# Layer norm with four neighbouring nodes to a partition, flat group buffers, earlier self copies and an earlier release of the second stage

## The reference, cut to what matters

```python
def layer0(x):                                   # GIN with batch norm
    agg = segment_sum(x[src], dst)
    z = relu(((1 + eps) * x + agg) @ W1 + b1) @ W2 + b2
    z = (z - mean(z, axis=0)) * rsqrt(var(z, axis=0) + 1e-5) * gamma + beta
    return z + x
def layer1(x):                                   # graph convolution
    return relu(segment_sum(edge_weight * x[dst], src) @ W3)
x = layernorm(x + layer0(x))                     # over the 256 features of a node
x = layernorm(x + layer1(x))
```

## Time and profile before

| | us |
|---|---|
| median of 3 runs | 4353.71 (4353.64 to 4358.59) |
| the profiled execution, its own time | 4363.42 |
| its span | 4361.6 |
| POOL busy | 3205.9 (74%) |
| PE busy | 3410.1 (78%) |
| DVE busy | 2603.8 (60%) |
| ACT busy | 413.7 (9%) |

### The profile page before, as it was taken

How to read it: one execution, slowest core, us unless ns; L and a number is a source line. 1 busy time by engine, 2 the same in 40 slices (tenths; PEclk the granted TensorE clock), 3 DMA queues, 4 the chain that set the end, 5 groups by cost and what they waited for, 6 DMA issues and landing times.

```text
span 4361.6 us, 69515 instructions
## 1 busy us (share of the span) xinstructions
PE 3410.1 (78%) x16117; PEld 2809.4 (64%) x16118; DVE 2603.8 (60%) x5750; ACT 413.7 (9%) x1049; POOL 3205.9 (74%) x3456
## 2 busy tenths in 40 slices
PE   2887877877887787778536888888888888888887
PEld 2776766666676676667435666666666666666666
DVE  3987877877888788788374434344334344344343
ACT  0000000000000000000151000000000000000001
POOL 6777777777777777777626777777777777777775
PEclk6998988988989898898758999999999999999998
DMA  4344444444444444444683343433434434434343
GB/s 146 114 119 118 121 118 116 121 118 119 118 118 117 119 120 119 115 121 118 189 288 108 113 118 117 119 117 118 120 115 120 120 115 120 120 115 119 115 120 99
DMA packets 305380, 540.19 MB, mean 124 GB/s; under 512 B 85290, under 2 KB 197790, under 8 KB 305326
## 3 DMA queue, kind: packets, MB, share of 16 engines
q0 software_dynamic: 159424, 434.52, 34.4%
q10 hardware_dynamic: 90884, 70.85, 5.3%
q1 hardware_dynamic: 55018, 34.16, 2.6%
HBM read 489.80 MB, written 46.88 MB: 123 GB/s over the span
## 4 chain that ended last, share of the span: by engine, by line
POOL 65%; issue 22%; PE 7%; DMA 3%; POOLq 1%; DVE 1%; ACT 1%; ACTq 0%; SPq 0%; DVEq 0%; PEldq 0%
POOL ring L612 32%; POOL ring L545 32%; PE ps L1290 3%; PE ps L1498 2%; DMA x_dram<-ring 1%; PE ps L1373 1%; DMA ring<-x_dram,idx 1%; POOLq L621 1%; DMA ring<-in_x,idx 1%; DMA z_dram<-z_pair 1%; ACT ring L1731 1%; POOL ring L558 0%; POOLq L622 0%; PE ps L1340 0%; POOLq L396 0%
## 5 line engine op out<-in xcount | busy, mean ns | idle before, releaser
L545 POOL DMA_INDIRECT ring<-in_x,idx x1664 | 1593.4, 958 | 504.2 <-issue 473.3
L612 POOL DMA_INDIRECT ring<-x_dram,idx x1612 | 1528.5, 948 | 551.3 <-issue 490.2
L1498 PE MATMUL ps<-ring,work 128*128 x6448 | 1523.7, 391 | 342.2 <-SPq L521 339.8
L1498 PEld LDWEIGHTS ps<-ring,work 128*128 128x128 f32 x6448 | 1218.4, 193 | 633.1 <-issue 475.2
L1160 DVE TENSOR_SCALAR work<-ps,dstT,wT 128x256 f32<-128x256 f32 x1612 | 741.8, 534 | 1134.0 <-PE ps L1498 1068.6
L1290 PE MATMUL ps<-ring,ones_sb 128*128 x3324 | 913.5, 423 | 362.9 <-SPq L454 325.0
L1290 PEld LDWEIGHTS ps<-ring,ones_sb 128*128 128x128 f32 x3324 | 679.0, 211 | 513.4 <-issue 413.3
L1373 PEld LDWEIGHTS ps<-work 128*128 128x128 f32 x3384 | 429.3, 197 | 18.5 <-DVE work L882 3.7
L1373 PE MATMUL ps<-work 128*128 128x128 f32 x3384 | 427.9, 279 | 2.5 <-DVE work L882 2.5
L897 DVE SCALAR_TENSOR_TENSOR ones_sb<-ps,tile_base,dstT 128x256 f32<-128x256 f32 (+1 forms) x294 | 311.7, 1099 | 57.3 <-PE ps L1273 31.9
L877 DVE TENSOR_TENSOR work<-ps,current 128x768 f32<-128x768 f32 x282 | 266.6, 945 | 10.8 <-PE ps L1373 10.8
(11 more groups left out here) (240 smaller groups left out, 2123.7 us busy)
## 6 DMA issues: line engine op xcount, KB each, us to landing
ring<-in_x,idx POOLq DMA_INDIRECT x1664
ring<-x_dram,idx POOLq DMA_INDIRECT x1612
z_dram<-z_pair ACTq DMA_DIRECT2D x49, 256.0 KB
ones_sb<-x_dram ACTq DMA_DIRECT2D x49, 256.0 KB, 3.6
ring<-z_dram SPq DMA_DIRECT2D x24, 512.0 KB, 5.8
ring<-in_x SPq DMA_DIRECT2D x24, 512.0 KB, 7.1
x_dram<-ring ACTq DMA_DIRECT2D x24, 512.0 KB, 3.7
out<-ones_sb ACTq DMA_DIRECT2D x48, 256.0 KB
```

The lines of the kernel that those rows point to most:

```text
L545: nc.gpsimd.indirect_dma_start(out=ring[:, q, c, :], out_offset=None, in_=x, in_offset=bass.IndirectOffsetOnAxis(ap=idx[:, q, c:c + 1], ax ...
L612: nc.gpsimd.indirect_dma_start(out=ring[:, q, c, :], out_offset=None, in_=x1_dram, in_offset=bass.IndirectOffsetOnAxis(ap=idx[:, q, c:c + ...
L1498: last = nc.tensor.matmul(to[:, t * D:(t + 1) * D], ones_of[:, b, c, t * P:(t + 1) * P], ring[:, ds((p + b) & (RING - 1), 1), c, :].rearra ...
```

## The change

- **Self copies**: in the first round POOL copies the first two quarters' self weights after 32 gathers, and each later quarter's behind its own gathers, in place of all four behind the 64th.
- **Four neighbours**: in a group, partition p holds the nodes 4p to 4p + 3 (2p, 2p + 1 in the last group), so that x is loaded and x1 stored in pieces of 4 KB. The group buffers are flat in the ring's memory. z stays transposed in z_dram, two pairs to a group: keep_z writes pieces of 2 KB, a group's load reads 4 KB a partition. PE picks every fourth column when it turns z back.
- **Slots**: group g uses slot (g + 7) mod 8.
- **Square root**: ACT takes one square root at its start; the batch norm's square root stands ahead of the last keep_z.
- **Second stage**: PE gives the credit for s_added2 at its start, not after W3; ACT loads W3 in the first stage, behind the loads of the staged lists.

```diff
-        z_group = tiles[:, 0:XBUFS * GROUP, :]
-        x_group = tiles[:, XBUFS * GROUP:2 * XBUFS * GROUP, :]
+        ring_flat = ring_rows[:, :, :, :].rearrange("p a c d -> p (a c d)")
+        z_group = ring_flat[:, 0:XBUFS * GROUP * D].rearrange("p (g m f n) -> p g m f n", g=XBUFS, m=GROUP // 2, f=KH)
+        x_group = ring_flat[:, XBUFS * GROUP * D:2 * XBUFS * GROUP * D].rearrange("p (g t d) -> p g t d", g=XBUFS, t=GROUP)
+        zn = ones_flat[:, 0:2 * GROUP * D].rearrange("p (b f n) -> p b f n", b=2, f=KH)
...
+        FIRST_SLOT = XBUFS - (NG - XBUFS) % XBUFS
+        def slot_of(g):
+            return (g + FIRST_SLOT) & (XBUFS - 1)
+        def x_tile(g, t):
+            return x_group[:, ds(slot_of(g), 1), t, :].rearrange("p a d -> p (a d)")
...
             def load_group(g):
+                at, size = slot_of(g), GROUP if g < NG - 1 else LG
+                rows = min(N - g * GROUP * P, size * P) // size
                 sp.wait_ge(s_zkept, 16 * -(-(g * GROUP + size) // 2))
+                sp.dma_start(z_group[:, at, 0:size // 2, :, :].rearrange("p m f n -> p (m f n)"),
+                             z_dram[g, :, 0:size // 2, :].rearrange("p m n -> p (m n)")).then_inc(s_zbuf[g % XBUFS], 16)
+                sp.dma_start(x_group[0:rows, at, 0:size, :].rearrange("p t d -> p (t d)"),
+                             x[g * GROUP * P:g * GROUP * P + rows * size, :].rearrange("(p t) d -> p (t d)", t=size)).then_inc(s_xbuf[g % XBUFS], 16)
...
                     for c in range(2):
                         gather(q, c)
-            pool.wait_ge(s_selves, 1)
-            for q in range(0, RING, QUARTER):
-                selves_of(q, selfT)
+                    if q == HALF - 1:
+                        pool.wait_ge(s_selves, 1)
+                        selves_of(0, selfT)
+                        selves_of(QUARTER, selfT)
+                    elif q > HALF and (q + 1) % QUARTER == 0:
+                        selves_of(q + 1 - QUARTER, selfT)
...
             pe.sem_inc(s_quarter, PARTS)
+            pe.sem_inc(s_added2, RING)
...                                                     # turn_group
-                        last = nc.tensor.transpose(ps[:, half * GROUP + t, m * P:(m + 1) * P], zn[:, half, t, m * P:(m + 1) * P], ident[:, :])
+                        last = nc.tensor.transpose(ps[:, half * GROUP + t, m * P:(m + 1) * P],
+                                                   zn[:, half, m, 0:size * P].rearrange("p (n t) -> p t n", t=size)[:, t, :], ident[:, :])
...
-            pe.sem_inc(s_added2, RING)                  # ahead of bucket(0, 0, 0)
...                                                     # ScalarE
+            act.wait_ge(s_const, 4)
+            nc.scalar.activation(lsd[:, 0:1], norm_eps[:, 0:1], ACT.Sqrt, bias=norm_eps[:, 0:1])
...                                                     # keep_z
-                act.dma_start(z_dram[ds(m * 2, 2), :, :].rearrange("t p (f n) -> p f t n", f=KH),
-                              z_pair[:, ds(m & 1, 1), :, :].rearrange("p a f (t n) -> p (a f) t n", t=2)).then_inc(s_zkept, 16)
+                act.dma_start(z_dram[ds(m >> 1, 1), :, ds(m & 1, 1), :].rearrange("a p m n -> p (a m n)"),
+                              z_pair[:, ds(m & 1, 1), :, :].rearrange("p a f n -> p (a f n)")).then_inc(s_zkept, 16)
...
             act.dma_start(all_runs[:, FORE:NS, :], stage_dram[FORE:NS, :, :].rearrange("s p n -> p s n")).then_inc(s_back[1], 16)
+            act.dma_start(w3s, w3.rearrange("(k p) n -> p k n", p=P)).then_inc(s_w3, 16)
             two_tiles(NS + 1, 5, False, False)
...
             z_out(k)
-            keep_z(k)
             act.wait_ge(s_bn, KH)
             nc.scalar.activation(zsd[:, :], zmv[:, :, 1], ACT.Sqrt, bias=norm_eps[:, 0:1]).then_inc(s_bnsd, 1)
+            keep_z(k)
...                                                     # keep_x1
-                act.dma_start(x1_dram[ds(g * (GROUP * P), size * P), :].rearrange("(t p) d -> p t d", p=P),
-                              x_group[:, ds((g & (XBUFS - 1)) * GROUP, size), :]).then_inc(s_x1_kept[half], 16)
+                act.dma_start(x1_dram[ds(g * (GROUP * P), size * P), :].rearrange("(p t) d -> p (t d)", p=P),
+                              x_group[:, ds(slot_of(g), 1), 0:size, :].rearrange("p a t d -> p (a t d)")).then_inc(s_x1_kept[half], 16)
...
             act.wait_ge(s_list2, N_INDICES)
-            act.dma_start(w3s, w3.rearrange("(k p) n -> p k n", p=P)).then_inc(s_w3, 16)
```

More of the change, by code:

```diff
@@ L81, in gnn @@
     LG = NT - (NG - 1) * GROUP
-    assert NG % 2 == 1 and NG > XBUFS
+    assert NG % 2 == 1 and NG > XBUFS and LG == 2 and (N - (NG - 1) * GROUP * P) % LG == 0
     ctx = ExitStack()
@@ L469, in load_group @@
             def load_group(g):
-                buf = (g % XBUFS) * GROUP
-                size = GROUP if g < NG - 1 else LG
+                at, size = slot_of(g), GROUP if g < NG - 1 else LG
+                rows = min(N - g * GROUP * P, size * P) // size
                 sp.wait_ge(s_zkept, 16 * -(-(g * GROUP + size) // 2))
[L473 to L481, removed]
+                sp.dma_start(z_group[:, at, 0:size // 2, :, :].rearrange("p m f n -> p (m f n)"),
+                             z_dram[g, :, 0:size // 2, :].rearrange("p m n -> p (m n)")).then_inc(s_zbuf[g % XBUFS], 16)
+                sp.dma_start(x_group[0:rows, at, 0:size, :].rearrange("p t d -> p (t d)"),
+                             x[g * GROUP * P:g * GROUP * P + rows * size, :].rearrange("(p t) d -> p (t d)", t=size)).then_inc(s_xbuf[g % XBUFS], 16)
+                return 16
             want, total = {}, [0] * XBUFS
@@ L547, in gather, with selves_of @@
                     in_offset=bass.IndirectOffsetOnAxis(ap=idx[:, q, c:c + 1], axis=0)).then_inc(s_gathered[q // QUARTER], 16)
+            def selves_of(q, of):
+                nc.gpsimd.tensor_copy(ring_self[:, q:q + QUARTER, :], of[:, q:q + QUARTER, :]).then_inc(s_selfed, 1)
             pool.wait_ge(s_first, 16)
@@ L1079, in affine_high @@
                     stand(dve)
-                some = slice(0, size)
-                mine = ds((g & (XBUFS - 1)) * GROUP, size)
-                nc.vector.tensor_scalar(zn[:, half or 0, some, P:D], z_group[:, mine, P:D],
+                nc.vector.tensor_scalar(zn[:, half or 0, 1, 0:size * P].rearrange("p (m n) -> p m n", m=size // 2),
+                                        z_group[:, ds(slot_of(g), 1), 0:size // 2, 1, :].rearrange("p a m n -> p (a m) n"),
                                         scale[:, 1:2], shift[:, 1:2], ALU.mult, ALU.add).then_inc(s_zn_high, 1)
@@ L1089, in add_group @@
                     stand(dve)
-                    mine = x_group[:, at_group(g, t), :].rearrange("p a d -> p (a d)")
+                    mine = x_tile(g, t)
                     nc.vector.scalar_tensor_tensor(
@@ L1744, in affine_low @@
                     stand(act)
-                mine = ds((g & (XBUFS - 1)) * GROUP, size)
-                nc.scalar.activation(zn[:, half, 0:size, 0:P], z_group[:, mine, 0:P],
+                nc.scalar.activation(zn[:, half, 0, 0:size * P].rearrange("p (m n) -> p m n", m=size // 2),
+                                     z_group[:, ds(slot_of(g), 1), 0:size // 2, 0, :].rearrange("p a m n -> p (a m) n"),
                                      ACT.Identity, bias=shift[:, 0:1], scale=scale[:, 0:1]).then_inc(s_zn, 1)
```

12 lines of the change are left out of this document (3 added, 9 removed).

## The result

The changed kernel takes 4329.53 us (median of 4 runs, 4326.83 to 4331.85), the kernel before 4353.68 (4351.92 to 4358.59, 4 runs beside it). The ratio is 0.9942, with an interval of 0.9927 to 0.9957: 24.2 us faster, with 18.7 to 31.8 in the interval.

A forecast was written before the change was run, and what follows sets the result against it. The prediction took the pace at which POOL issues gathers as the bound, gains coming only where POOL stands still: 9.1 + 10.4 + 10 + 8.6 = 38.1 us off 4353.7 gives 4315.6 us, range 4308 to 4334.

The forecast's parts named there:

- Self copies: First gather round: POOL's stand of 8.92 us for PE before gather 65 goes, gaining 9.1 us (8.9 to 9.3).
- rival 1: Stores take as long as before, so the layer norm's middle gains 0: 22.0 us in all, 4331.7 us; chance 0.14.
- Square root at the start, W3 early: ACT's early square root and W3's load in the first stage are covered by other work: zero.
- From the last sum to the layer norm: From PE's last sums to the first affine, with shorter z stores and no table load: 10.4 us (4.3 to 11.0).
- a store at 4 to 4.5 us: Layer norm's start: with a quarter of the pieces, z stores of 7.41, 8.00 and 7.36 us fall to this length.
- the part called sure: Layer norm's start: the wait behind the aggregates and the table load go, the lower bound of 4.3 us.
- The layer norm itself: First to last x1 store, 118.97 us for 24 steps: faster stores gain 10 us (0 to 13.4).
- with 4 KB pieces the store no longer starts behind two long loads: Layer norm's middle: the step by which x1's stores, at 5.89 us, land sooner; 4.6 us needed for 13.4 us.
- Release: Start of the second stage: POOL's first gather no longer waits for PE and W3, gaining 8.6 us (8.0 to 9.3).
- 2 (a deeper queue): Layer norm's start: second z store waits behind all 8 MB of loads, 3.4 us lost; total gain 14.3, 4339.4; chance 0.04.
- 3 (stepped reads): Layer norm: PE's reads of every fourth float bound it; at four times the cost 4396 us, slower; chance 0.05.
- 4: Second stage's start: the release does nothing, since POOL waits for x1 or the indices anyway: 4324.2 us; chance 0.04.

The follow-up runs named there:

- hold: Changed kernel, SP asking for two groups, then the other six only once the third-last z store has landed: 5433.89 us, ratio 0.9929 to the kernel before.
- hold_b: The same edit as hold, run again on a second chip: 5390.66 us, ratio 0.9978 to the kernel before.
- best: Changed kernel with the edits of hold and lead6, and the last keep_z behind ACT's first two affines: 5440.15 us, ratio 0.9946 to the kernel before.
- best_b: The same edits as best, run again on the second chip: 5383.58 us, ratio 0.9966 to the kernel before.
- sqrt_only: Kernel before with only the square root at the start and the last z store behind the batch norm's square root: 4350.44 us, ratio 0.9993.
- release_only: Kernel before with only PE's credit for s_added2 at its start and W3 loaded in the first stage: 4344.08 us, ratio 0.9976.
- self_only: Kernel before with only the self copies moved earlier: 4345.69 us, ratio 0.9981.
- lead6: Changed kernel, SP reporting one group further ahead and ACT's store waiting for the store two groups before: 5440.18 us, ratio 0.9944 to the kernel before.
- lead6_b: The same edit as lead6, run again on the second chip: 5375.52 us, ratio 0.996 to the kernel before.
- layout_only: Kernel before with only the four-neighbour layout, flat buffers, longer pieces and slot order: 4345.7 us, ratio 0.9982.

## Why the prediction was right and where it was off

Two of its four terms came out, and the two that hang on shorter stores did not. The measured time lies in the range only because the range had been drawn out to rival 1: the forecast's own range of 4311 to 4328 misses it by 1.5 us, and the 38.1 us lie outside the measured interval. The prediction's own sign of being wrong, stores of 6 us, is what the trace shows. That the number came as near as 14 us is owed to the parts that have nothing to do with the layout.

**Self copies** (9.1 us): right. 9.1 alone in its trace, 10.0 in the profile after, where the first round's gathers also ended some 0.9 us sooner.

**Square root at the start, W3 early** (zero): right. Self copies and release bring their full terms with it, and in the second stage's group no gather waits for PE.

**From the last sum to the layer norm** (10.4 us): wrong in size, 6.0 us. The step that failed is "a store at 4 to 4.5 us". It took the slow store to be a matter of many pieces in the queue. The pieces did become fewer, SP's issues took 11.2 us where "under 10" was expected, the last of them 1.20 us long and not 1.66, yet the stores took 5.51, 7.32 and 6.54 us. What shortened them was fewer loads ahead: in hold, hold_b, best and best_b the third is issued 9.7 to 9.9 us behind the first, in the four traces on these chips with all eight groups asked for at once 11.5 to 13.1, with the same pieces. A second, smaller fault is in the part called sure: the moved keep_z waits ahead of the affine (ACT starts it 1.1 us behind DVE here, and stands 2.24 us for the store in sqrt_only), an instruction queued behind a wait on its own engine that the prediction should have named.

**The layer norm itself** (10 us): wrong, -1.5 us, within what traces of unchanged middles differ by (119.0, 120.4, 121.0 and 121.6 in before, release_only, self_only and sqrt_only). The failed step is "with 4 KB pieces the store no longer starts behind two long loads". It does start behind them. In the profile after, a store is issued at 2173.91, behind the four loads that SP issued from 2169.40 to 2171.60. The DMA queues by windows of 1 us (packets, MB, share; q1 is SP's, q10 ACT's), for those that begin at 2175, 2176, 2177 and 2178:

```profile
q1 hardware_dynamic: 95, 0.34, 86.2%
...
q1 hardware_dynamic: 100, 0.39, 95.6%
...
q10 hardware_dynamic: 2, 0.01, 2.0%
...
q10 hardware_dynamic: 83, 0.34, 81.5%
q1 hardware_dynamic: 34, 0.08, 20.7%
...
q10 hardware_dynamic: 57, 0.18, 44.6%
```

For 3 us after its issue the store moves 2 packets, while SP's loads take the engines; by 2178 the windows hold the whole 2.1 MB of the four loads. Then the store moves its 0.5 MB almost alone, within 2 us, and SP learns of its landing at about 2180.2. Before it was the same with the short pieces: the store issued at 2195.96 moved nothing until the window of 2199, behind four loads issued from 2191.43 on. The bandwidth rose where the first groups were loaded (375 to 412 GB/s; 375 to 381 in the four traces with the old layout, 409 to 417 in five with the new one, whose buffers are flat too), but 1 MB at 412 in place of 375 GB/s is 2.5 us in place of 2.8, and that went into no shorter store.

The term had a second fault, in its upper end of 13.4 us: DVE's pace through the whole layer norm was read as 4.56 us a group at its end. In lead6, lead6_b, best and best_b, which have a group more of lead, a period is 4.86 or 4.87 us in the mean of 18 and the middle is 111.3 to 114.4 us, not 105.6. Even with the stores that it assumed, some 7.7 us were there to be gained (119.0 to 111.3), and not 10.

The "Specifications" rule of "DMA: Bandwidth & Descriptors" in the Trainium skill, 512 bytes and up at line rate, gave rival 1's outcome, and its outcome came. The trace doesn't bear out its reason in full: with pieces of 4 KB and flat buffers the loads moved 10% faster than with pieces of 1 KB, and no run tells these two apart. The same page's section "Queues, rings and completion order" says that an engine takes turns between the queue rows that have work, packet by packet. By that the store would have had a share from its start; the windows show it almost absent for 3 us. Once a store's packets come beside loads, the trace agrees: in the window of 2138 a z store issued at 2133.86 moved 0.14 MB beside 0.26 MB of loads. The windows don't say whether its packets waited to be made or waited in a ring.

**Release** (8.6 us): right, 8.7 in the profile and 8.9 alone.

**Sum.** The terms that failed are 4.4 and 11.5 us too large, together 15.9; the forecast was 13.9 too low. The 2.0 us between are within the runs.

**Rivals.** 1 (stores as long as before, 22.0 us) is what happened, with 24.2 us: that stores of x1 don't get shorter with the pieces is shown by the chain and by layout_only. Its chance of 0.14 was too low. SP's late issues, the row held against it, were indeed a matter of pieces (21.7 us for the sixteen before, 11.2 after), but they didn't tell how long a store takes. 2 (a deeper queue) has something in it, since the second z store is the longest, 7.32 us, but it lost nothing against the 8.00 before. 3 (stepped reads) is out: eight transposes take 1.98 us, against 1.97 for adjacent columns, both at a granted clock of 0.50, the 1.2 GHz level. By "SBUF — State Buffer", section "Door 1: The DMA port swizzle", of the Trainium skill they would have become dearer; at a step of 16 bytes this trace shows no such price on PE. 4 is out by release_only.

## What to carry to other kernels

A store that takes several times its data's time under prefetch should be looked at in 1-us windows of the queues before its pieces are made longer: if its packets are absent and another queue's fill the engines, fewer loads issued ahead of it or one more step of lead are what shortened the stretches here, and its layout is not; ask also what comes last once they are shorter, here the lists. When a wait is moved behind another instruction, follow it to what is queued behind it now. A term worked out as "the other engine's limit" is an upper end, and its pace is to be read where it does the loop's whole work (4.86 us a group, not 4.56); the middle of a loop that is bound by latency gives back nothing when only the rate rises.

## What the runs showed of the hardware that was not expected

- Longer pieces (1 KB to 4 KB in the loads and in x1's stores) with flat buffers raised the loads from 375 to 412 GB/s and made x1's stores no shorter: 5.05 us before, 5.13 after, in the mean from the store to SP's next load.
- A store behind loads of the other queue moved 2 packets in the first 3 us after its issue; the z stores' median over the whole kernel, mostly with no such loads, is 2.7 us (after).
- Reads by PE with a step of 16 bytes cost as much as adjacent ones, 1.98 us for eight transposes.
- The stores of x1 bunch in pairs, 3.97 us apart and then 6 to 9 us, before and after: two stores land some 1.2 us apart, so two groups' loads are issued together, and the next store stands behind both.
